# Attention on one core: ScalarE multiplies one chunk of the probabilities by its factors, GpSimd takes another one over from VectorE

## The reference, cut to what matters

```
K = einsum('bpd,ihd->biph', x, W_K)      # x: 1 x 2048 x 128, 16 heads of 64
Q = einsum('bpd,ihd->biph', x, W_Q)
V = einsum('bpd,ihd->biph', x, W_V)
scores = where(tril, einsum('biph,biqh->biqp', K, Q), -1e10)
attn = softmax(scores / 8, axis=-1)
z = einsum('biph,biqp->biqh', V, attn)
out = einsum('bqf,df->bqd', z_flat, W_O)
x = x + out
```

## Time and profile before

| what | value |
|---|---|
| median of 3 runs | 1289.68 us (1289.42 to 1291.8) |
| the profiled execution | 1289.25 us |
| its span, first to last instruction | 1287.5 us |
| mean granted TensorE clock over the span | 0.948 |
| attention, steady part | about 27 to 960 us of the span |

### The profile page before, as it was taken

The page is one execution under the profiler, slowest core; times in us unless marked ns, Lnnn a source line. Parts: engine busy times, 40 slices in busy tenths (PEclk is TensorE's granted clock), DMA queues, the critical chain, the costliest instruction groups (busy, mean ns, idle before and its releaser), DMA issues. The chain is left out here.

```text
span 1287.5 us, 24496 instructions
## 1 busy us (share of the span) xinstructions
PE 1162.6 (90%) x8058; PEld 860.6 (67%) x8058; DVE 931.6 (72%) x2059; ACT 791.8 (61%) x2189; POOL 833.7 (65%) x797
## 2 busy tenths in 40 slices
PE   5899999999999999999999999999996393997385
PEld 4577677677767767776777677677765391554385
DVE  5878878878787788788777877887854463767454
ACT  5777677767777776777777777766742262322153
POOL 1678677858766786778586677867792463563443
PEclk9999999999999999999999999999996695998588
DMA  4100800170043008002600530010050121000123
GB/s 122 43 2 1 154 4 2 34 128 2 1 105 53 1 9 153 1 2 50 108 1 1 118 45 1 18 50 2 2 148 18 54 61 39 1 1 1 34 64 98
DMA packets 74452, 55.66 MB, mean 43 GB/s; under 512 B 7925, under 2 KB 63225, under 8 KB 74329
## 3 DMA queue, kind: packets, MB, share of 16 engines
q1 hardware_dynamic: 71832, 48.96, 18.4%
q0 software_dynamic: 2496, 5.13, 1.2%
HBM read 13.29 MB, written 24.01 MB: 29 GB/s over the span
## 5 line engine op out<-in xcount | busy, mean ns | idle before, releaser
L387 DVE TENSOR_REDUCE at_nmax<-at_ps 128x1 f32<-128x512 f32 (+3 forms) x640 | 374.0, 603 | 126.2 <-PE at_ps L555 123.2
L359 POOL TENSOR_SCALAR at_prob<-at_prob,at_scale 128x512 f32<-128x512 f32 (+3 forms) x312 | 428.0, 1387 | 1.8
L552 PE MATMUL at_ps<-at_k_st,at_q_parts 128*128 128x512 f32 (+3 forms) x640 | 283.5, 443 | 4.9 <-DVE at_k_st L443 2.6
L469 ACT ACTIVATE at_prob<-at_ps,at_nmax 128x512 f32<-128x512 f32 (+3 forms) x416 | 259.1, 630 | 45.7 <-DVE at_nmax L387 43.6
L581 PE MATMUL at_ps<-at_probT,at_v 128*64 128x256 f32 (+1 forms) x2304 | 270.3, 374 | 1.4 <-DVE at_probT L410 1.3
L555 PE MATMUL at_ps<-at_k_st,at_q_parts 128*128 128x512 f32 (+3 forms) x640 | 252.9, 395 | 0.0
L482 ACT ACTIVATE at_probT<-at_ps 128x512 f32<-128x512 f32 (+1 forms) x288 | 165.0, 573 | 140.8 <-PE at_ps L566 129.6
L359 POOL TENSOR_SCALAR late<-late,at_scale 128x512 f32<-128x512 f32 (+1 forms) x168 | 225.8, 1358 | 1.6
L410 DVE COPY at_probT<-at_ps 128x512 f32<-128x512 f32 (+1 forms) x288 | 189.0, 656 | 50.9 <-PE at_ps L566 48.4
L566 PE MATMUL at_ps<-ident,at_prob 128*128 128x128 f32 x1440 | 219.6, 274 | 2.9 <-DVE at_probT L410 1.8
L581 PEld LDWEIGHTS at_ps<-at_probT,at_v 128*64 128x64 f32 x2304 | 152.5, 136 | 102.1 <-issue 40.9
(11 more groups left out here) (200 smaller groups left out, 1503.4 us busy)
## 6 DMA issues: line engine op xcount, KB each, us to landing
at_q_parts<-at_q_parts SPq DMA_DIRECT2D x64, 256.0 KB, 3.7
slots_in<-zeros SPq DMA_DIRECT2D x6, 1483.5 KB, 16.5
slots_in<-zeros SPq DMA_DIRECT2D x6, 1419.0 KB, 15.6
f_xs<-slots_in SPq DMA_DIRECT2D x46, 64.5 KB
late<-in_L_ffn_w_dram SPq DMA_DIRECT2D x1, 2048.0 KB, 9.0
late<-in_L_ffn_w_dram SPq DMA_DIRECT2D x4, 512.0 KB, 6.1
f_got<-slots_out SPq DMA_DIRECT2D x8, 256.0 KB, 3.6
out_dram<-x SPq DMA_DIRECT2D x4, 256.0 KB, 2.4
```

The lines of the kernel that those rows point to most:

```text
L359: pool.tensor_scalar(cols, cols, scale[:, k, u, c:c + 1], None, ALU.mult).then_inc(s_fix["pool"], 1)
L387: dve.tensor_reduce(nmax[:, q % 2, 2 * i + h, c:c + 1], bank, AX.X, ALU.max, negate=True).then_inc(s_max, 1)
L469: act.activation(prob[ROW_HOME[j]][u][:, c * BANK:c * BANK + w], ring[use_of["score", p, j, i, h, c] % RING][:, 0:w], ACT.Exp, bias=nmax[: ...
L552: pe.matmul(bank[:, 0:w], q_hi[h][:, r * P:(r + 1) * P], keys, start=True, stop=False)
```

## The change

Who multiplies which chunk, for each row:

- The first chunk (c = 0) of the first head's second tile (h = 0, i = 1) goes from POOL to ACT: one fix a row, 64 in all, of 512 columns in 56 and 256 in 8.
- The fourth chunk (c = 3) of the second head's second tile (h = 1, i = 1), which only rows 6 and 7 have, goes from DVE to POOL: 16 in all, 8 of 512 columns and 8 of 256. The other chunks of that unit stay with DVE.

The planner is told the length of an ACT fix, and that ACT prefers it to evicts. PE and POOL wait on one more semaphore.

```diff
-    def fixer(h, i):
-        return "dve" if h == 1 and i == 1 else "pool"
+    def fixer(h, i, c):
+        if (h, i, c) == (0, 1, 0):
+            return "act"
+        return "dve" if h == 1 and i == 1 and c < NC - 1 else "pool"
...
-                    length = {"pool": 0.28 + 1.28 * w, "dve": 0.1 + 0.5 * w}[fixer(h, i)]
-                    step(("fix", p, j, c, h, i), fixer(h, i), length, ("pool", "scale", p, j))
+                    length = {"pool": 0.28 + 1.28 * w, "dve": 0.1 + 0.5 * w, "act": 0.2 + 0.45 * w}[fixer(h, i, c)]
+                    step(("fix", p, j, c, h, i), fixer(h, i, c), length, ("pool", "scale", p, j))
...
-                     *[(fixer(h, i), "fix", p, j, 2 * g // TPC, h, i) for i in range(2)])
+                     *[(fixer(h, i, 2 * g // TPC), "fix", p, j, 2 * g // TPC, h, i) for i in range(2)])
...
-              "act": ["factor", "leave", "evict", "vproject", "high", "exp"],
+              "act": ["factor", "leave", "fix", "evict", "vproject", "high", "exp"],
...
-                            pool.wait_ge(s_fix["dve"], count_of["dve", "fix", p2, j2, chunks(j2) - 1, 1, 1])
+                            pool.wait_ge(s_fix["dve"], count_of["dve", "fix", p2, j2, min(chunks(j2), NC - 1) - 1, 1, 1])
+                            pool.wait_ge(s_fix["act"], count_of["act", "fix", p2, j2, 0, 0, 1])
...
+                    elif kind == "fix":
+                        _, _, j, c, h, i = it
+                        q = place[p, j]
+                        k, u, w = q % 2, 2 * i + h, width(j, i, c)
+                        act.wait_ge(s_scale, q + 1)
+                        cols = prob[ROW_HOME[j]][u][:, c * BANK:c * BANK + w]
+                        act.activation(cols, cols, ACT.Copy, scale=scale[:, k, u, c:c + 1]).then_inc(s_fix["act"], 1)
...
-                            e = fixer(h, i)
+                            e = fixer(h, i, 2 * g // TPC)
```

More of the change, by code:

```diff
@@ L290, in attention @@
         s_low, s_gap, s_factor, s_part, s_total, s_rinv = (sem(n) for n in ("s_low", "s_gap", "s_factor", "s_part", "s_total", "s_rinv"))
-        s_scale, s_fix = sem("s_scale"), {e: sem("s_fix_" + e) for e in ("pool", "dve")}
+        s_scale, s_fix = sem("s_scale"), {e: sem("s_fix_" + e) for e in ("pool", "dve", "act")}
         s_turn = [sem(f"s_turn{h}") for h in range(2)]
```

## The result

| | before | changed |
|---|---|---|
| median, 8 runs each | 1289.75 us | 1293.05 us |
| lowest and highest | 1289.42 to 1291.8 | 1292.2 to 1296.51 |
| the profiled execution's span | 1287.5 us | 1290.4 us |

The ratio is 1.0027, interval 1.0017 to 1.0036: 0.3% slower, 3.5 us by the ratio.

A forecast was written before the change was run, and what follows sets the result against it. PE was taken to bound the kernel by its list's distances plus its waits; 4.6 + 0.5 - 1.3 - 1.0 + 0.5 = +3.3, with small waits +4, gave 1293.5 us, forecast's own range 1292.3 to 1296, whole range 1289 to 1298.

The forecast's parts named there:

- Turns of the second head too close, +4.6: PE's turns of the second head stand closer than 1.47 us at 25 places instead of 16: +4.6 us.
- the start of row 7 in the last pair, +0.5: The add with four small instructions holds DVE 1.14 us, so the evict of g = 1 delays the waiting value: +0.5 us.
- Place A: Pairs 3, 5, 7: DVE has a maximum before the evict, so the second head's next turn loses 0.84 us each, 2.5 us.
- Place C: Pairs 2, 4, 6: the second head's next turn waits for its evict, at 4 and 6 behind a low step: 0.6 us each.
- The first turn, -1.3: Start of the attention: ACT's fix runs beside POOL's, so the first turn starts about 47.7 us instead of 49.2: -1.3 us.
- Scores that wait for low steps: In pairs 2 and 5 a score waited 0.5 us for a low step; the new lists have other steps there: -1.0 us.
- DMA, 0 with 1 either way: The queries' DMA is just in time or late in both kernels: 0, with 1 us either way.
- PE's own list, 0 with 1 either way: Same PE instructions with other neighbours; distances differ by under 0.5 us in sum: 0, with 1 us either way.
- Waits that eat each other, up to -2: Where PE comes later to a wait it had anyway, one eats the other: taken as 0, up to -2 us.
- No change: Rival, 1290.5 us: the second head's new waits fall where PE would wait anyway for DMA or a low step; chance 0.18.
- Faster: Rival, 1286.4 us: late fixes hold the kernel, and POOL's 77 us less give all 2.9 us back; chance 0.06.
- Much slower: Rival, about 1298 us: ACT's in-order fix waits for POOL's scale and passes waits on to PE; chance 0.14.

The follow-up runs named there:

- the second trace: The changed kernel measured once more, unedited, against the kernel before: 1293.48 us, ratio 1.0023.
- POOL's part alone: Against the kernel before, only the fourth chunk of rows 6 and 7 goes from DVE to POOL, with new lists: 1291.68 us, ratio 1.0014.
- the fix two steps later: Lists of before with the new split, ACT's fix two steps ahead of the row's first evict instead of four, against the kernel before: 1295.44 us, ratio 1.0037.

## Why the prediction was right, and where it was off

The forecast was 1293.5 us, slower with 0.75, and the result is 1293.05. Its mechanism stands on three legs: the work alone, in the old order, costs nothing that shows (1.0003, at most 1.0013); the changed kernel with PE's list moved in twelve places gets more than half of the loss back (1.0007, and 2.5 of 3.7 us in the trace); and the waits are seen one by one at the places that were foretold. Step by step:

- *Engines' work is no time by itself.* Right: POOL 76.4 us less (77 foretold), ACT 36.2 more (38). *DVE 8 to 11 less* was wrong, it was 3.4. The busy time per fix rose from 584 ns (93.4 us in 160) to 615 (88.5 in 144), which eats 4.5 us. What lengthens a fix is open; what it isn't is shown below.
- *ACT's fix 0.6 us.* Measured 0.72, outside the 0.55 to 0.7 that I gave. The price for ACT's progress was right all the same, since the next instruction starts 0.61 to 0.63 behind it; ACT's busy rows overlap too. By the Trainium skill, VectorE: DVE Perf Modes, section on the TRN2 errata, the estimate was 0.61; as a duration the trace says more.
- *Turns of the second head too close, +4.6, and the start of row 7 in the last pair, +0.5.* Foretold 5.1 together, measured +5.8. Place A is exact (1.64 foretold, 1.63 measured, 0.84 lost, three pairs), so is row 6 (0.35 in six pairs), and row 7 has 0.94 for 0.48 before. Place C was mis-sized: 0.6 each foretold, 0.8 and twice 0.94 measured, 0.9 us more in all. At p = 2 the low step ends 0.81 us behind the start of the turn (370.65 to 371.46), where I had taken about 0.5, so the evict starts 0.85 behind it and the distance is 1.68, not 1.5.
- *The first turn, -1.3.* The step that failed most. The start at 47.60 is as foretold (47.7), in part by luck, as the second trace has 49.23; the price isn't: 0.5 came of it, since what stood ahead of the turn, hidden in the wait, now stands behind it. The 1.3 that I took left room for a wait for exps, and none for this work.
- *Scores that wait for low steps, -1.0.* Right, -1.1 (1.4 to 0.3). *For exps, +0.5*: nothing by my count, though the profile's label for it goes from 0.5 to 1.1 us. *DMA, 0 with 1 either way*: -1.3, just outside; of the 0.85 us at the first score of p = 6 0.35 is left, which the count books on the low step.
- *PE's own list, 0 with 1 either way.* +1.3 by the table, just outside; by the two other choices of the usual distance +3.9 or +1.7, so it was not nothing, and its size is the least certain of all.
- *Waits that eat each other, up to -2, and 0 to 1.5 on top for small ones.* Together -1.1. The attention's later start adds +0.3, which nothing of the change brought about.

The measured terms add up to 5.8 + 1.3 - 0.5 - 1.1 - 1.3 - 1.1 + 0.3 = +3.4, and the last out step moved by +3.5. So the total of +4 was near in part by luck, because misses cancelled: evicts and PE's own distances cost 2.0 more than I said and the first turn gave 0.8 less, while the DMA (1.3), the exps (0.5) and small waits (1.1, where the +4 had 0.7 on top) came out 3.6 better.

The rivals. *No change*: it needed half of the waits hidden; they weren't. *Faster*: it would have needed DVE to get to its evicts sooner because POOL is less busy. The line's view of DVE's fixes in the changed kernel, against the earlier trace rows:

```profile
L420 DVE TENSOR_SCALAR at_prob<-at_prob,at_scale x96: 353/658/999, 57.2 to 953.8; 128x512 f32<-128x512 f32 x80, 128x256 f32<-128x256 f32 x16
```

They have become longer, not shorter. The busy time per fix is 584 ns with POOL busy for 678 us, 615 with 602, 580 in the kernel with the old lists (605), 574 with POOL's part alone (693): it doesn't follow POOL's load, and with the lists kept it hardly moves at all (584 to 580) while POOL's load falls by 73 us. The rule of the Trainium skill, SBUF — State Buffer, section Who interferes with whom, which would have made this rival, is not refuted as a rule by that (which fixes meet which of POOL's instructions depends on the lists); as a gain from less work on POOL it doesn't show here. *Much slower*: ACT waits for the scale 5.1 us in 11 cases, but in the changed kernel no first turn of a row is over 0.06 us late with the end of ACT's fix just ahead of it. The run with the fix two steps later shows what a late fix costs (1.0037).

What stays open: what sets the length of a DVE fix, how PE's own distances, 1.3 us longer by the table, split over its neighbours, and why other planner numbers give better lists. A second bank for the turns of a head, the direct cure, wasn't tried, as all eight banks are taken.

## What to carry to other kernels

Where a planner sets the order, a change in who does what is first of all a new list for the engine that bounds: compare that list with the old one, look for steps on the same buffer that have come too close (here 1.47 us from turn to turn, 1.64 with another job ahead of the evict), and price each from the trace. To tell work from order, run the new work in the old order. And before you move work, compare the lengths that the planner is told with the distances from start to start in the trace: the lists that came of it were worth two to four times as much here as this change cost. A single change of a length proves little, though: 0.04 us in one of them moved the kernel as much as the change did.

## What the runs showed of the chip

- ACT takes 723 ns to multiply 512 columns in SBUF in place by a factor per partition (509 for 256 columns), against 598 for its evict of 512 columns from PSUM. By start distances both are cheaper, 0.61 to 0.63 us for the fix, since the next instruction begins about 0.1 us ahead of the end that the trace shows; for the evict it is 0.48 to 0.49 us.
- An exp of 512 columns with its sum takes 0.69 us, the readout of the sum another 0.20, and yet the next exp starts 0.66 behind the first: adding durations overstates ACT by a third.
- The bank's turnaround hardly varies: the turn starts 0.14 us behind the end of DVE's evict at place A and at place C and 0.15 in the earlier trace rows, and 0.15 at nearly all the other evict waits of both kernels.
- The label of a wait can name the wrong engine: POOL for the turn at 401.61, whose POOL fix had ended 4.9 us earlier, and POOL or issue for the 9.0 us at 17 places that end just behind ACT's fix in the kernel with the fix two steps later.
- Chips differ by 0.2% (1287.5 and 1290.5 us for the same kernel), as much as the change under study makes: only ratios on one chip can be compared.
